# Without a wait: POOL's additions of batch two beside the normalisation of batch zero

## What is computed

```python
x = x + 0.5 * moe(layernorm(x), Wr, br, W1, b1, W2, b2)   # 8 experts, 2 chosen for each token, hidden 512
x = x + mamba(layernorm(x), in_proj_w, conv_w, ...)       # projections, causal conv, scan, output norm
x = x + 0.5 * moe(layernorm(x), Wr, br, W1, b1, W2, b2)
```

## Time and profile before

| | us |
|---|---|
| median of 3 runs | 423.59 |
| lowest and highest | 421.11, 424.4 |
| profiled execution | 421.09 |
| its span, first to last instruction | 419.3 |

### The profile page before, as it was taken

How to read it: one execution, slowest core, us unless ns; L and a number is a source line. 1 busy time by engine, 2 the same in 40 slices (tenths; PEclk the granted TensorE clock), 3 DMA queues, 4 the chain that set the end, 5 groups by cost and what they waited for, 6 DMA issues and landing times.

```text
span 419.3 us, 8909 instructions
## 1 busy us (share of the span) xinstructions
PE 330.8 (79%) x2366; PEld 294.6 (70%) x2366; DVE 269.0 (64%) x920; ACT 209.8 (50%) x501; POOL 220.7 (53%) x263
## 2 busy tenths in 40 slices
PE   8784799986698198799999999749469998778800
PEld 7684799976697185567777779739459998767700
DVE  4883477753465178768788986899447775345416
ACT  3832456644464065736657573453245665455402
POOL 4026355566545177274656879651644556654512
PEclk9578899999899598899999999877899999899965
DMA  6791111111111410000000000010111111111154
GB/s 161 239 283 45 27 39 42 40 44 44 41 33 33 172 48 2 1 0 2 1 2 3 0 0 2 2 74 28 52 31 39 38 41 45 41 40 38 33 172 147
DMA packets 18674, 22.23 MB, mean 53 GB/s; under 512 B 4114, under 2 KB 13508, under 8 KB 18628
## 3 DMA queue, kind: packets, MB, share of 16 engines
q1 hardware_dynamic: 13092, 11.18, 8.9%
q0 software_dynamic: 4096, 8.40, 6.7%
q10 hardware_dynamic: 1440, 2.11, 1.4%
HBM read 14.33 MB, written 7.34 MB: 52 GB/s over the span
## 4 chain that ended last, share of the span: by engine, by line
PE 51%; DVE 11%; issue 9%; DMA 6%; SPq 6%; ACT 5%; POOL 4%; another core or an unknown queue 3%; DVEq 3%; ACTq 0%; POOLq 0%
PE PS L793 16%; PE PS L805 16%; SPq L401 3%; PE PS L842 3%; PE PS L849 3%; PE PS L896 2%; PE PS L814 2%; PE PS L778 2%; DMA YT_all<-y_rows 2%; SPq L395 2%; DMA y_rows<-YS,rows_out 2%; DVE X L1507 2%; POOL rs L501 2%; DVE YT_all L1475 1%
## 5 line engine op out<-in xcount | busy, mean ns | idle before, releaser
L479 POOL DMA_INDIRECT XG<-xn_rows,rows_in x64 | 62.1, 970 | 83.8 <-issue 35.7
L793 PE MATMUL PS<-XT_all,W1B 128*128 x624 | 90.1, 290 | 15.8 <-DVE XT_all L1454 8.0
L793 PEld LDWEIGHTS PS<-XT_all,W1B 128*128 128x128 f32 x624 | 80.3, 201 | 18.9 <-issue 18.2
L1121 ACT ACTIVATE H<-PS,W1B 128x128 f32<-128x128 f32 x156 | 48.7, 363 | 88.9 <-PE PS L793 60.7
L489 POOL DMA_INDIRECT y_rows<-YS,rows_out x64 | 62.3, 974 | 48.3 <-issue 18.9
L805 PE MATMUL PS<-H,W2B 128*128 128x128 f32 x624 | 85.3, 281 | 0.5 <-issue 0.5
L805 PEld LDWEIGHTS PS<-H,W2B 128*128 128x128 f32 x624 | 78.4, 197 | 0.9 <-issue 0.6
L1484 DVE COPY W2B<-W2S 128x513 f32 x78 | 35.5, 455 | 39.1 <-DVE YT_all L1475 26.6
L1111 ACT ACTIVATE W1B<-W1S 128x516 f32 x78 | 49.4, 633 | 21.7 <-issue 9.0
L1475 DVE TENSOR_SCALAR YT_all<-PS,W2B 128x128 f32 x78 | 27.2, 349 | 43.3 <-PE PS L805 25.8
L1465 DVE TENSOR_SCALAR H<-PS,W1B 128x128 f32<-128x128 f32 x156 | 46.9, 342 | 6.4 <-PE PS L793 3.8
(11 more groups left out here) (204 smaller groups left out, 556.0 us busy)
## 6 DMA issues: line engine op xcount, KB each, us to landing
YT_all<-y_rows SPq DMA_DIRECT2D x8, 512.0 KB, 5.1
W1S<-in_L_ffn_W SPq DMA_DIRECT2D x1, 2048.0 KB
W2S<-in_L_ffn_W SPq DMA_DIRECT2D x8, 256.0 KB
xn_rows<-XN ACTq DMA_DIRECT2D x8, 256.0 KB, 4.4
X<-in_L_attn_x SPq DMA_DIRECT2D x4, 256.0 KB, 4.7
XG<-xn_rows,rows_in POOLq DMA_INDIRECT x64
y_rows<-YS,rows_out POOLq DMA_INDIRECT x64
out_x<-X SPq DMA_DIRECT2D x4, 256.0 KB, 2.3
```

The lines of the kernel that those rows point to most:

```text
L479: g.indirect_dma_start(out=XG[:, u, :], out_offset=None, in_=xn_dram, in_offset=bass.IndirectOffsetOnAxis(ap=rows_in[:, i:i + 1], axis=0), ...
L793: last = mm(PS[2 + 2 * half + j % 2][:, c * P:(c + 1) * P], W1B[w][:, h * P:(h + 1) * P], XT_all[:, ds(start, P)], start=True, stop=True)
L1121: last = A(H[w][:, 2 + c, :], PS[4 + j % 2][:, c * P:(c + 1) * P], ACT.Relu, bias=W1B[w][:, HID + 2 + c:HID + 3 + c])
```

## The change

The wait of POOL between the root of batch zero and the additions of batch two is taken out. Nothing else differs.

```diff
@@ -509,7 +509,6 @@
                 st.link(add_output(0, 1, 1))
                 add_output(1, 1, 2).then_inc(s_comb_pool, 1)
                 root0(0)
-                wait_xn(pool, 0)
                 st.link(add_output(0, 2, 3))
                 add_output(1, 2, 4).then_inc(s_comb_pool, 1)
                 root0(1)
```

## The result

The change makes the kernel slower by 0.9%. Over 20 runs each the median went from 426.33 to 430.20 us; the ratio is 1.0089, with a 95% interval from 1.0052 to 1.0126, which is 2.2 to 5.4 us, 3.8 in the middle. The ratio compares only the runs within 1.5% of the fastest of their kernel, so it isn't quite that of the two medians. The forecast was 425.6 us with a range of 422.6 to 427.8, so the time lies above the range; that it would stay within 1% was right, narrowly. The profiled execution has a span of 427.5 us (its run 429.26).

A forecast was written before the change was run, and what follows sets the result against it. ACT's XN of batch one was taken to wait on two nearly tied paths, POOL's adds and batch zero; two XN stopped by adds make it 2.0 us later, so 423.59 + 2.0 = 425.6 us, range 422.6 to 427.8.

The forecast's parts named there:

- stay within 1%: Whole kernel: measured time within 1% of before, 4.2 us; chance 0.91, against 0.07 for slower and 0.02 for faster.
- The start of the adds: POOL, batch two: first add starts where the root of batch zero ends, at about 151.3, with no wait, 1.26 us earlier.
- two stopped XN: DVE, batch zero: POOL's two adds each hold one XN, 1.1 to 1.4 us each; XN done 2.1 us later; chance 0.5.
- POOL's idle time moved: POOL: after its adds end at 153.94 it waits 1.9 us for DVE's statistics of batch one, before that batch's root.
- the shift held by the add of batch three: DVE, batch one: shift still held by POOL's add of batch three, ending at 158.4, 0.65 us later than before.
- the slack of the path of batch zero: ACT's XN of batch one: its tap ends only 0.13 to 0.17 us before that XN, so earlier adds gain about 0.1 us.
- The first rival: DVE, batch zero: XN runs beside POOL's add unstopped, giving 423.5 us, no slower; chance 0.2.
- PE's line of the sum: PE and ACT, batch zero: transposes at 154.65, first projection at 156.05, tap from 158.96 to 159.74, each 2.1 us later.
- the clock comes on top: PE under projections 0 and 1: idling lowers its clock, costing at most 1.7 us more, +3.7, 427.3 us; chance 0.15.
- I find nothing that swallows 2 us: From the time steps to the kernel's end: one chain, so the whole 2.0 us delay reaches the span.
- The level: Starting time for the whole kernel: 423.59 us, the median of three runs, to which 2.0 us were added.
- the 2.0 of the sum: ACT's XN of batch one starts at 159.8 against 157.81, so time steps and span come 2.0 us later.

The follow-up runs named there:

- a_accum: Changed kernel with XN of batches zero and three in the tensor_scalar form that also writes a result per row; total 1.0023 of before.
- a_fill32b: Second profile of the changed kernel with 32 filler matmuls in place of 26; 22.5 us from ACT's first gating to DVE's first time step; total 1.0003.
- b_gap: Kernel before, wait kept, with 16 filler matmuls in place of 26; ratio 1.0007, 21.6 us from ACT's first gating to DVE's first time step.
- a_accum_order: Changed kernel with XN writing a result per row, and PE's projection of block 1 ahead of the time steps of batch zero; total 0.9987 of before.
- a_one: Changed kernel with POOL's wait put back one add later, between the two adds of batch two; total 1.0033 of before.
- a_look4: Changed kernel unedited, fifth profile, on a chip where the kernel before took 400.8 us; single run 403.33 us.
- a_look5: Changed kernel unedited, sixth profile, on a chip where the kernel before took 400.8 us; single run 404.50 us.

## Why the forecast missed

**What held.** The start of the adds, two stopped XN of 1.3 and 1.4 us, XN of batch zero 2.0 us later (3.18 us after the root, before 1.15), POOL's idle time moved and grown to 1.9 us, the shift held by the add of batch three (1.22 us), and the slack of the path of batch zero too small to take any of it. The first rival (XN passes beside the add) is refuted in every profile of the changed kernel, and a_accum shows when it would have been right.

**The step that failed** is PE's line of the sum: transposes, first projection and tap each "with the same 2.1". It let PE idle for 2 us and then took every duration behind that from before. In all four profiles of the changed kernel on the first chips the clock fell behind that idle time: the forecast had ACT's XN of batch one 2.0 us later after the first gating, measured are 3.2 to 4.5 us, and 1.8 where the clock held. This was the rival "the clock comes on top", with a chance of 0.15. It named the place rightly, and its +3.7 us fit the 3.8 us in total and the 3.2 to 3.8 in the distance; but that is in part luck, since three of its terms were off and the errors cancel:

- the stops cost the distance 1.6 us and not 2.0. The sentence "I find nothing that swallows 2 us" overlooked ACT's wait of 0.58 us for the shift of batch two;
- the four profiles lose 2.5 to 3.1 us to the clock, against 22.5 us in a_fill32b, which has no low stretch in the distance; the rival put a new stretch at 1.3 to 1.7;
- before's own distance holds a low stretch, worth about 0.9 us by the estimate above. In three of the four profiles projection 2 and its transposes run at full clock. The rival had named this as possible, and gave it no number.

Together: 1.6 - 0.9 and 2.5 to 3.1 on top, that is 3.2 to 3.8 us.

**The level** was the other half of the miss. The forecast stood on a median of three, 423.59; over 20 runs the kernel before has 426.33. Of the 4.6 us between 425.6 and 430.2, 2.7 are this, and 1.9 are what the change cost beyond the 2.0 of the sum. The upper end of the range lay 4.2 us above the median of three; the change itself, 3.9 us between the two medians of 20, would have been inside that.

**What is open.** Why the clock falls behind 1.5 to 2.3 us of idle time in the changed kernel and not behind 2.0 in b_gap, or behind 1.5 in a_accum_order. Idle time up to 1.15 us ahead of the transposes (a_one, both profiles with 32 fillers, a_look4 and a_look5) was never followed by it in that place. But idle time of PE can't be all: before's low stretch under projection 2 begins at about 162, where no idle time of PE in the 15 us ahead of it is longer than 0.97 us. The experiments show that filling the idle time takes the loss away (no low stretch there in three profiles out of three), not what sets the clock.

## To carry to other kernels

A wait between two engines may be what keeps their instructions apart. Before it is taken out, look whether the two that then overlap belong to the kinds that stop each other, whose path is the tighter one, and whether the waiting side has other ways to be undisturbed (here, another form of the same instruction). And where TensorE is made to wait longer, move its fillers with it: the clock took at least as much as the stops themselves.

## What I had not expected of the hardware

- A tensor_scalar from SBUF to SBUF with two scalar columns takes 0.34 us alone and 1.30 and 1.41 beside POOL's adds; the form that also writes a result per row takes 0.40 us alone or beside them. The Trainium skill ("SBUF — State Buffer", "Who interferes with whom") excepts just this form, and the trace agrees.
- 52 filler matmuls last 7.5 to 8.8 us, depending on how long the clock stays low after the wait for the outputs, so a fixed number of fillers ends at a different time in each execution.
- The same kernel took 400.8 us on one chip and 414 to 430 on others. The two expert layers take 90 us each there against 103 to 110, a part of which is given back in the waits for their outputs; the mixer takes the same time.
